# Attention logits and token logits in groups of the TensorE array, second feed-forward product of unsplit fp32 operands

## Chip, cores and metric

The kernel runs on one core of a Trainium2 chip. The metric is the device time in microseconds (us) of one execution; each figure is a median of several runs.

## What is computed

Eight sequences of 750 frames of 192 channels go through four stages. The reference, cut to what matters here:

```python
h = relu(pointwise(depthwise(x)));  h = pairs_max(h)              # 750 -> 375 tokens
h = layernorm(real(fft2(h)))
w = layernorm(h) @ w_qkv                                          # 12 heads of 64
logits = sum((w / norm)**2, -1) * temp;  Pi = softmax(logits)     # "token logits", 12 x 375
h = h - (w * Pi / (1 + sum(Pi * w*w))) @ w_out
probs = softmax(q @ kk.T / 4)                                     # 12 heads of 16, for 56 selected tokens
attn = probs @ v @ Wo;  h2 = layernorm(h) + where(selected, attn, mix)
out = h2 + gelu(n2 @ W1 + bf1) @ W2 + bf2                         # 192 -> 768 -> 192
```

All of it is fp32 in and out.

## The kernel before

The work is pipelined over the eight batches. Each engine has its own instruction stream, and `pipeline` calls `step(p, q, r, w)` ten times in it: batch p is in the front part (convolution, spectrum, token attention), batch q in the middle part (normalisation, scores, routed attention), batch r in the last part (feed-forward), and w is the batch whose depthwise taps VectorE works on ahead of time. Six of the ten steps have a front, a middle and a last batch; below they are "full steps". Step 0 has only a front, step 1 front and middle, step 8 middle and last, step 9 only the last. The order within a step is written out by hand for each engine, and engines wait for one another through semaphores.

The 375 tokens lie in three tiles of 125 partitions or along the free dimension; the 768 inner columns of both feed-forward and token attention are six tiles j of 128.

Where a product needs more precision than one pass, an operand is split into a high and a low part (type fp32r), and three products high·high, high·low and low·high are summed (`split_product`, L1068). An unsplit fp32 product is one call, which the trace shows as two records of matmul.

What the change touches, in the order of a full step:

- `gelus` (ScalarE, L985): after each `forward_up(r, j)` the gelu goes into one of three buffers (L989), then a copy of it becomes the high part (L993). `split_gelu` (GpSimd, L789 to 796) subtracts to get the low part. Between its pieces GpSimd works the `power` calls (L802), the reciprocal roots of the norms, for VectorE.
- On VectorE `spectrum_norm` (L432) and `second_norm` (L444, tile `even`) run meanwhile. TensorE's `front_input(p)` transposes `even` (L1060); ScalarE and VectorE split the result (L879, L451).
- `logits(q, j)` (TensorE, L1248): 96 channels x (2 heads x 64 queries) against 375 keys, six calls. The operand `qb` (VectorE, L618) holds the queries under a mask, so that each call sees only its two heads among six. The results alternate between two PSUM banks, so call j waits for the exponential j-2.
- For each j the loop then runs `qkv(p, j)` (L1126), a `logits` call and `turn(q, j-1)` (L1258, transposes of the probabilities). ScalarE does, per j, the exponential (L962), two copies of the qkv result (L888, L889) and the copy of the turned probabilities (L967). VectorE does the maxima (L625) and two depthwise taps after every second one (L371).
- `forward_down(r, 0, j)` (L1321): three split products per j, for token tile 0. Tiles 1 and 2 follow further down in the step.
- `token_logits(p)` (L1132): six calls of 12 output rows x 375 columns, accumulated in one PSUM region, after `rhead` (VectorE, L463). VectorE takes the maximum (L468) after two more depthwise taps, ScalarE the exponential (L893) after the copy of the last turned tile, VectorE the softmax (L473 to L484), and TensorE spreads the result over the heads (`spread`, L1143).
- `values` (L1266) already puts its products of 32 output rows into three groups of columns of the array.
- `token_out` (L1151): eighteen unsplit fp32 calls of 128 x 125 weights and 192 columns.

In step 0 GpSimd also splits the weights (`split_weight`, L782), `w_2` among them, while VectorE does taps.

## Time and profile before

| | us |
|---|---|
| median of 3 runs | 689.04 (688.39 to 697.84) |
| the profiled execution, its own time | 688.68 |
| its span from first to last instruction | 686.7 |
| TensorE busy in the span | 585.2 (85%) |
| VectorE busy | 475.2 (69%) |
| ScalarE busy | 255.3 (37%) |
| GpSimd busy | 144.4 (21%) |
| chain that ended last: TensorE, VectorE, GpSimd | 51%, 21%, 5% of the span |

The profiled execution lies 0.4 us under the median, and 2.0 us of it lie outside the span. The granted clock of TensorE was 0.925 in the mean: it has two levels, 1.2 and 2.4 GHz, and the profile writes the mean of a stretch as a share of the higher one. The busy time of a group of matmuls counts overlapping records once, so a mean duration is the latency of one record and not what it costs in a row of them; what it costs is read from the starts.

### The profile page before, as it was taken

The numbers are of one execution on the slowest core, as the hardware profiler recorded it, in microseconds if no ns is written. First come the engines' busy times: TensorE is split into PE (matmuls) and PEld (weight loads), VectorE is DVE, ScalarE is ACT, GpSimd is POOL, SyncE is SP. The second block draws the span as 40 slices with busy tenths as digits, with TensorE's granted clock in tenths as the row PEclk, the third lists the DMA queues.
The fourth block names the chain that finished last, engine by engine and source line by source line (L and its number), as shares of the span: only waits on it lengthen the run. The fifth ranks groups of instructions, "written<-read, shape, count | busy, mean of one in ns | idle before, by whom it ended". The sixth has DMA issues, their size and how long they took to land.

```text
span 686.7 us, 9949 instructions
## 1 busy us (share of the span) xinstructions
PE 585.2 (85%) x3488; PEld 470.3 (68%) x3488; DVE 475.2 (69%) x1235; ACT 255.3 (37%) x662; POOL 144.4 (21%) x126
## 2 busy tenths in 40 slices
PE   1536598989989998999899999999899989968975
PEld 1325276759776876787777787678768776866765
DVE  6549767667886888678878878788768573843330
ACT  0013113701474146603671267116721564115431
POOL 5228011002050025002500231032202040023022
PEclk9976698877999999999999999999899999958978
DMA  7420010010001000100000000100000000000000
GB/s 181 117 70 1 0 35 1 1 34 1 1 0 36 17 1 2 35 6 12 0 27 7 17 0 0 34 17 0 0 0 17 1 0 1 18 2 0 1 18 17
DMA packets 8325, 12.50 MB, mean 18 GB/s; under 512 B 1875, under 2 KB 6957, under 8 KB 8296
## 3 DMA queue, kind: packets, MB, share of 16 engines
q1 hardware_dynamic: 8296, 12.12, 6.6%
q8 instruction: 17, 0.28, 0.2%
q14 instruction: 12, 0.10, 0.0%
HBM read 9.81 MB, written 2.30 MB: 18 GB/s over the span
## 4 chain that ended last, share of the span: by engine, by line
PE 51%; DVE 21%; issue 18%; POOL 5%; ACT 3%; DMA 1%; POOLq 0%; DVEq 0%; SPq 0%; ACTq 0%
PE xb L1068 7%; PE yb L1321 6%; PE xb L1151 5%; PE xb L1132 5%; PE zb L1068 5%; PE zb L1248 5%; PE yb L1068 3%; PE xb L1098 3%; PE zb L1258 2%; DVE even L444 2%; POOL gelu_low L795 2%; DVE dw L389 2%; POOL rs L805 2%; DVE st L342 2%; PE xb L1143 2%
## 5 line engine op out<-in xcount | busy, mean ns | idle before, releaser
L805 POOL TENSOR_TENSOR rs<-ve,half 125x3 f32<-125x3 f32 (+1 forms) x32 | 33.6, 1049 | 390.8 <-DVE ve L354 318.1
L371 DVE SCALAR_TENSOR_TENSOR dw<-x_in,w_dw_sb,dw 96x750 f32<-96x750 f32 x84 | 82.7, 1033 | 0.2
L795 POOL TENSOR_TENSOR gelu_low<-gelu,gelu_high 128x375 fp32r<-128x375 f32 x48 | 47.2, 998 | 119.7 <-ACT gelu_high L993 119.5
L1068 PE MATMUL yb<-n2T,w_sb 96*128 96x376 f32 x288 | 64.1, 370 | 5.5 <-DVE n2T L684 5.0
L1068 PE MATMUL xb<-xhT,w_qkv_sb 96*128 96x376 f32 x288 | 64.5, 370 | 1.2 <-DVE xhT L451 1.2
L1068 PEld LDWEIGHTS yb<-n2T,w_sb 96*128 96x128 f32 x288 | 53.5, 208 | 8.4 <-DVE n2T L684 5.7
L1068 PEld LDWEIGHTS xb<-xhT,w_qkv_sb 96*128 96x128 f32 x288 | 53.0, 205 | 5.7 <-DVE xhT L451 3.0
L1151 PE MATMUL xb<-scratch,w_sq 128*125 128x192 f32 x288 | 53.0, 347 | 4.1 <-ACT scratch L900 4.1
L1321 PE MATMUL yb<-w_sb,gelu_high 128*125 128x192 f32 x288 | 53.5, 287 | 2.3 <-POOL gelu_low L795 2.3
L1151 PEld LDWEIGHTS xb<-scratch,w_sq 128*125 128x125 f32 x288 | 51.2, 203 | 5.0 <-DVE scratch L512 4.5
L1321 PEld LDWEIGHTS yb<-w_sb,gelu_high 128*125 128x125 f32 x288 | 44.2, 194 | 8.3 <-issue 5.7
L625 DVE TENSOR_REDUCE nmax<-zb 128x1 f32<-128x375 f32 x48 | 25.6, 544 | 24.8 <-PE zb L1248 24.4
L1248 PE MATMUL zb<-kT,qb 96*128 96x375 f32 x96 | 41.0, 526 | 1.3 <-ACT probs L962 1.3
L1321 PE MATMUL yb<-w_sb,gelu_low 128*125 128x192 f32 x144 | 40.0, 278 | 0.0
L1132 PE MATMUL xb<-w_sq,rhead 128*12 128x375 f32 x96 | 33.9, 505 | 7.1 <-DVE rhead L463 7.1
L967 ACT ACTIVATE probsT<-zb 125x384 f32<-125x384 f32 x48 | 24.9, 518 | 39.8 <-PE zb L1258 39.8
L1098 PE MATMUL xb<-dft_n_sb,pooled_h 125*96 125x376 f32 x96 | 33.8, 504 | 0.9 <-DVE pooled_h L400 0.9
L490 DVE TENSOR_TENSOR w_sq<-w_s,xb 128x376 f32<-128x376 f32 x48 | 25.2, 538 | 11.5 <-PE xb L1143 11.5
L983 ACT ACTIVATE n2T<-zb 96x750 fp32r<-96x750 f32 x8 | 6.3, 791 | 68.1 <-PE zb L1060 68.1
L900 ACT ACTIVATE scratch<-w_out_sb,natt 128x192 f32<-128x192 f32 x24 | 9.2, 445 | 59.9 <-DVE natt L510 59.9
L1258 PEld LDWEIGHTS zb<-ident_sb,probs 128*125 128x125 f32 x144 | 22.5, 187 | 12.9 <-issue 4.8
L1088 PE MATMUL xb<-w_pw_sb,dw 97*125 97x192 f32 x64 | 17.9, 364 | 14.5 <-DVE dw L389 13.9
(188 smaller groups left out, 1269.5 us busy)
## 6 DMA issues: line engine op xcount, KB each, us to landing
x_in<-in_x SPq DMA_DIRECT2D x8, 567.0 KB, 4.2
out<-res_f SPq DMA_DIRECT2D x8, 281.2 KB
probsT<-in_w_qkv SPq DMA_DIRECT2D x1, 576.0 KB, 6.9
w_out_sb<-in_w_out SPq DMA_DIRECT2D x1, 576.0 KB
probs<-in_w SPq DMA_DIRECT2D x1, 576.0 KB
probsT<-in_w SPq DMA_DIRECT2D x1, 576.0 KB, 4.3
rows_sb<-in_rows SPq DMA_DIRECT2D x1, 504.0 KB
dft_n_sb<-in_dft_n SPq DMA_DIRECT2D x1, 493.5 KB
```

The costliest lines, as they stand in the source:

```text
L371: ins = dve.scalar_tensor_tensor(out=dw[0:C, c, :], in0=src, scalar=w_dw[:, c, k:k + 1], in1=dw[0:C, c, :], op0=ALU.mult, op1=ALU.add)
L490: dve.tensor_tensor(u[:, j, :], w_s[:, j, :], xb[:, j % 2, 0:NE], ALU.mult).then_inc(u_done.sem, 1)
L625: dve.tensor_reduce(nmax[:, j:j + 1], zb[:, j % 2, 0:N], AX.X, ALU.max, negate=True).then_inc(qmax_done.sem, 1)
L795: pool.tensor_tensor(gelu_low[:, j, 0:N], gelu[:, j % 3, 0:N], gelu_high[:, j, 0:N], ALU.subtract)\
L805: pool.tensor_tensor(out_[:], in_[:], half3[:] if len(in_.shape) == 3 else half3[:, 0, :], ALU.pow).then_inc(rs.sem, 1)
L1068: ins = mm(o, a[:, k], b[:, l], start=start and k + l == 0, stop=stop and k == 1)
L1098: ins = mm(xb[0:C, c, 0:2 * KF], pooled_h[:, t, chan(c)], dft_n[:, t, :], start=(t == 0), stop=(t == T - 1))
L1132: ins = mm(xb[0:H1, 0, 0:N], rhead[:, j, :], w_sq[:, j, 0:N], start=(j == 0), stop=(j == IT - 1))
L1151: ins = mm(o, u[:, j, tok(t)], w_oa[:, j, :], start=(j == 0), stop=(j == IT - 1))
L1248: mm(zb[:, j % 2, 0:N], qb[:, c, 2 * i:2 * i + 2, :].rearrange("p h q -> p (h q)"), kT[:, c, 0:N], start=True, stop=True).then_inc(ql_read ...
L1258: ins = pe.transpose(zb[0:P, 2 + j % 2, 128 * t:128 * t + 128], probs[:, j, tok(t)], ident[:])
L1321: ins = mm(o, g[:, j, tok(t)], w_2[:, l, j, :], start=(j == 0 and g is gelu_high and l == 0), stop=(j == IT - 1 and g is gelu_low))
```

## The change

The attention logits become two rounds of three calls. A call takes 32 rows of the array (two heads, their real 32 channels) instead of 96 masked ones, and the three calls of a round go to three groups of rows and to three PSUM banks (`score_bank`), two of which are banks that the feed-forward uses. The token logits go to four groups of columns: call j writes the 32 rows of group j % 4, so `rhead`, `head_mask`, the softmax tiles and the selector `head_sel` get 128 rows instead of 12 or 64; high and low part of Pi are now made in one operation on 128 rows. The gelu stays whole in six buffers, and `forward_down` is one fp32 call per j with the unsplit `w_2`; the high and low parts, their copies, subtractions and signals are gone. New waits: a round of `logits` waits for the gelu that read its feed-forward bank, and `forward_down(r, 0, 0)` for all exponentials of q. The diff, cut to its core:

```diff
-        head_sel = sb("head_sel_sb", [64, IT, 128], fp32r)
+        low_rows = sb("low_rows_sb", [128, 1])
+        head_sel = sb("head_sel_sb", [128, IT, 128], fp32r)
-        w_2 = sb("w_2_sb", [128, 2, IT, D], fp32r)
+        w_2 = sb("w_2_sb", [128, IT, D])
-        rhead = sb("rhead", [128, IT, H1])
+        rhead = sb("rhead", [128, IT, 32])
-        qb = sb("qb", [C, CT, H1 // 2, Q])
+        qb = sb("qb", [C, CT, 2, Q])
-        gelu = sb("gelu", [128, 3, NE])
-        gelu_high = sb("gelu_high", [128, IT, NE], fp32r)
-        gelu_low = sb("gelu_low", [128, IT, NE], fp32r)
+        gelu = sb("gelu", [128, IT, NE])
...
+        def score_bank(j):
+            return (zb[:, 0], zb[:, 1], yb[:, 0], yb[:, 1], zb[:, 0], zb[:, 1])[j]
...
             def token_max(b):
-                dve.tensor_reduce(lgm[:, 0:1], xb[0:H1, 0, 0:N], AX.X, ALU.max, negate=True).then_inc(lmax_done.sem, 1)
+                dve.tensor_reduce(lgm[:, 0:1], xb[:, 0, 0:N], AX.X, ALU.max, negate=True).then_inc(lmax_done.sem, 1)
...
+                dve.tensor_copy(pi_high[:], pi[:]).then_inc(pi_steps.sem, 1)
+                dve.wait_ge(*pi_steps.of(b, 5))
                 if not first(b):
                     dve.wait_ge(*pib_ready.before(b))
-                dve.tensor_copy(pi_parts[0:H1, :], pi[:]).then_inc(pi_steps.sem, 1)
-                dve.wait_ge(*pi_steps.of(b, 5))
-                dve.tensor_tensor(pi_parts[32:32 + H1, :], pi[:], pi_parts[0:H1, :], ALU.subtract).then_inc(pi_low_done.sem, 1)
+                dve.scalar_tensor_tensor(out=pi_parts[:], in0=pi_high[:], scalar=low_rows[:], in1=pi[:],
+                                         op0=ALU.mult, op1=ALU.add).then_inc(pi_low_done.sem, 1)
...
-            def split_gelu(b, j0, j1):
...
-                for j in range(j0, j1):
-                    pool.wait_ge(*gelu_high_done.of(b, j + 1))
-                    pool.tensor_tensor(gelu_low[:, j, 0:N], gelu[:, j % 3, 0:N], gelu_high[:, j, 0:N], ALU.subtract)\
-                        .then_inc(gelu_low_done.sem, 1)
...
-                    split_weight(2, w_2, w_2_32)
...
             def gelus(b, j):
                 act.wait_ge(*w1_ready.of(b, j + 1))
-                if j >= 3:
-                    act.wait_ge(*gelu_low_done.of(b, j - 2))
-                act.activation(gelu[:, j % 3, 0:N], yb[:, j % 2, 0:N], ACT.Gelu, bias=b_1[:, j:j + 1]).then_inc(gelu_done.sem, 1)
                 if j == 0 and not first(b):
                     act.wait_ge(*w2_ready.before(b))
-                act.wait_ge(*gelu_done.of(b, j + 1))
-                act.activation(gelu_high[:, j, 0:N], gelu[:, j % 3, 0:N], ACT.Copy).then_inc(gelu_high_done.sem, 1)
+                act.activation(gelu[:, j, 0:N], yb[:, j % 2, 0:N], ACT.Gelu, bias=b_1[:, j:j + 1]).then_inc(gelu_done.sem, 1)
...
             def token_logits(b):
...
                 for j in range(IT):
-                    ins = mm(xb[0:H1, 0, 0:N], rhead[:, j, :], w_sq[:, j, 0:N], start=(j == 0), stop=(j == IT - 1))
+                    g = j % 4
+                    ins = mm(xb[32 * g:32 * g + 32, 0, 0:N], rhead[:, j, :], w_sq[:, j, 0:N], start=(j < 4), stop=(j + 4 >= IT))
...
-            def logits(b, j):
...
+            def logits(b, c, r):
+                if c == 0:
+                    pe.wait_ge(*qb_done.of(b))
+                    pe.wait_ge(*ms_done.of(b))
+                else:
+                    pe.wait_ge(*prob_done.of(b, 2))
+                if r is not None:
+                    pe.wait_ge(*gelu_done.of(r, IT - 1 + c))
+                for i in range(3):
+                    rows32 = slice(32 * i, 32 * i + 32)
+                    ins = mm(score_bank(3 * c + i)[:, 0:N], qb[rows32, c, :, :].rearrange("p h q -> p (h q)"), kT[rows32, c, 0:N],
+                             start=True, stop=True)
+                ins.then_inc(ql_ready.sem, 1)
...
-            def forward_down(b, t, j):
+            def forward_down(b, t, j, q=None):
                 if t + j == 0:
-                    pe.wait_ge(*gelu_low_done.of(b))
+                    if q is not None:
+                        pe.wait_ge(*prob_done.of(q))
                     pe.wait_ge(*gelu_done.of(b))
...
-                for g, l in ((gelu_high, 0), (gelu_high, 1), (gelu_low, 0)):
-                    ins = mm(o, g[:, j, tok(t)], w_2[:, l, j, :], start=(j == 0 and g is gelu_high and l == 0),
-                             stop=(j == IT - 1 and g is gelu_low))
+                ins = mm(o, gelu[:, j, tok(t)], w_2[:, j, :], start=(j == 0), stop=(j == IT - 1))
...
                 if middle:
-                    logits(q, 0)
-                    logits(q, 1)
+                    logits(q, 0, r)
                 for j in range(IT):
                     if front:
                         qkv(p, j)
                     if middle:
-                        if 1 <= j < IT - 1:
-                            logits(q, j + 1)
+                        if j == 2:
+                            logits(q, 1, r)
                         if j:
                             turn(q, j - 1)
                 if last:
                     for j in range(IT):
-                        forward_down(r, 0, j)
+                        forward_down(r, 0, j, q)
```

## Rows read from the trace of the kernel before

**Rows 1.** Stretches: length, busy us (records) per engine, PEclk, DMA share, GB/s

```profile
303.32:374.70 71.38, 67.32 (x438) 54.51 (x437) 57.56 (x152) 31.50 (x83) 14.23 (x13) 1.00 0.05 12
446.10:520.22 74.12, 70.07 (x439) 56.98 (x438) 57.65 (x151) 32.41 (x83) 14.22 (x13) 0.95 0.01 4
520.22:592.97 72.75, 68.74 (x438) 55.59 (x437) 45.70 (x137) 32.14 (x83) 14.25 (x13) 0.98 0.02 5
```

**Rows 2.** Timeline, TensorE, a full step: start, us, line, operation [idle before, releaser]

```profile
341.72 0.84 PE L1060 MATMUL xb<-ident_sb,even 125*96 125x125 f32 x6 [1.82 <-DVE even L444]
...
350.01 0.79 PE L1248 MATMUL zb<-kT,qb 96*128 96x375 f32 x2
...
352.01 0.79 PE L1248 MATMUL zb<-kT,qb 96*128 96x375 f32 x2
...
356.38 3.95 PE L1132 MATMUL xb<-w_sq,rhead 128*12 128x375 f32 x12
360.26 0.59 PE L1258 MATMUL zb<-ident_sb,probs 128*125 128x128 f32 x3
...
363.74 0.61 PE L1143 MATMUL xb<-pi_parts,head_sel_sb 64*128 64x376 f32 x2 [0.94 <-DVE pi_parts L484]
```

**Rows 3.** Timeline, VectorE in step 1 and a full step, GpSimd in the latter

```profile
115.33 1.07 DVE L432 SCALAR_TENSOR_TENSOR res<-res,rs,rows_sb 125x192 f32<-125x192 f32 x3
...
118.84 0.96 DVE L444 TENSOR_SCALAR even<-res,ag,rs 125x192 f32<-125x192 f32 x3 [0.38 <-POOL rs L805]
...
334.36 1.95 DVE L432 SCALAR_TENSOR_TENSOR res<-res,rs,rows_sb 125x192 f32<-125x192 f32 x3
...
338.74 2.92 DVE L444 TENSOR_SCALAR even<-res,ag,rs 125x192 f32<-125x192 f32 x3 [0.38 <-POOL rs L805]
...
338.67 2.87 POOL L795 TENSOR_TENSOR gelu_low<-gelu,gelu_high 128x375 fp32r<-128x375 f32 x3
```

**Rows 4.** Timeline, ScalarE in the loop over j of that full step

```profile
345.19 0.57 ACT L962 ACTIVATE probs<-zb,nmax 128x375 f32<-128x375 f32 x1
...
348.31 0.61 ACT L962 ACTIVATE probs<-zb,nmax 128x375 f32<-128x375 f32 x1
...
350.04 0.65 ACT L962 ACTIVATE probs<-zb,nmax 128x375 f32<-128x375 f32 x1
...
354.95 0.21 ACT L889 ACTIVATION_READ_ACCUMULATOR w_sq<-xb 128x1 f32 x1
```

**Rows 5.** Chain that ended last, forward_down of tile 0: start, us, what

```profile
354.50 1.94 PE yb L1321 x18
```

**Rows 6.** Line view of token_out: min/median/max ns, first and last start

```profile
L1151 PE MATMUL xb<-scratch,w_sq x36: 325/327/346, 303.3 to 309.0; 128*125 128x192 f32 x36
```

**Rows 7.** Timeline, TensorE: `values`, three groups of columns

```profile
360.78 0.86 PE L1266 MATMUL zb<-probsT,v 125*32 125x128 f32 x18
```

**Rows 8.** Timeline, VectorE and ScalarE after the loop over j

```profile
355.78 1.90 DVE L371 SCALAR_TENSOR_TENSOR dw<-x_in,w_dw_sb,dw 96x750 f32<-96x750 f32 x2
...
361.28 0.55 ACT L893 ACTIVATE lg<-xb,lgm 12x375 f32<-12x375 f32 x1
```

**Rows 9.** Timeline, step 0: GpSimd splitting w_2, VectorE

```profile
56.40 2.85 POOL L787 TENSOR_TENSOR w_sb<-probs,w_sb 128x1152 fp32r<-128x1152 f32 x1
...
56.66 7.36 DVE L371 SCALAR_TENSOR_TENSOR dw<-x_in,w_dw_sb,dw 96x750 f32<-96x750 f32 x4
...
72.72 0.54 DVE L468 TENSOR_REDUCE lgm<-xb 12x1 f32<-12x375 f32 x1 [2.19 <-PE xb L1132]
```

**Rows 10.** Step 9: timeline of ScalarE; chain, all three tiles of forward_down

```profile
671.25 0.57 ACT L989 ACTIVATE gelu<-yb,b_sb 128x375 f32<-128x375 f32 x1
...
673.47 7.79 PE yb L1321 x54
```

**Rows 11.** Stretches of step 1, ahead of the spread and behind it

```profile
143.10:145.10 2.00, 0.00 (x0) 0.00 (x0) 1.61 (x6) 0.25 (x2) 0.00 (x0) 1.00 0.00 0
146.00:163.40 17.40, 17.40 (x72) 13.94 (x64) 12.05 (x41) 1.51 (x4) 0.96 (x1) 0.51 0.00 1
```

More of the change, by code:

```diff
@@ L106, in audio_tower @@
         rnrm = sb("rnrm", [128, IT])
-        rhead = sb("rhead", [128, IT, H1])
-        lg = sb("lg", [H1, NE])
-        lgm = sb("lgm", [H1, 4])
-        pi = sb("pi", [H1, NE])
-        pi_parts = sb("pi_parts", [64, NE], fp32r)
+        rhead = sb("rhead", [128, IT, 32])
+        lg = sb("lg", [128, NE])
+        lgm = sb("lgm", [128, 4])
+        pi = sb("pi", [128, NE])
+        pi_high = sb("pi_high", [128, NE], fp32r)
+        pi_parts = sb("pi_parts", [128, NE], fp32r)
         u = w_sq
@@ L246, in audio_tower @@
         qkvs = pieces(w_qkv32, "w_qkv")
-        heads = (pieces(head_mask, "head_mask") + pieces(temp, "temp") + pieces(head_sel32, "head_sel")
+        heads = (pieces(head_mask, "head_mask") + pieces(temp, "temp") + pieces(head_sel32, "head_sel") + pieces(low_rows, "low_rows")
                  + pieces(rows, "rows", slice(2, 8)))
         rests = [x for dst, name in (
-            (w_out, "w_out"), (w_k32, "w_k"), (w_v32, "w_v"), (w_m, "w_m"), (w_2_32, "w_2"), (w_q, "w_q"), (w_o, "w_o"),
+            (w_out, "w_out"), (w_k32, "w_k"), (w_v32, "w_v"), (w_m, "w_m"), (w_2, "w_2"), (w_q, "w_q"), (w_o, "w_o"),
             (b_k, "b_k"), (q_mask, "q_mask"), (parity, "parity"), (pair, "pair"), (fold, "fold"), (later, "later"), (slot, "slot"), (b_1, "b_1"),
             (nsT[C:C + 1, 0, :], "ones_q"), (cxT[C:C + 1, 0, :], "ones_q2")) for x in pieces(dst, name)]
-        MEMSETS, WEIGHTS = 5, 6
+        MEMSETS, WEIGHTS = 5, 5
         SPLIT = MEMSETS + 2 * WEIGHTS
-        FILLS, SELECTORS = 6, 7
+        FILLS, SELECTORS = 5, 6
         FIRST, DFT, NORM, QKV, HEAD, REST = (16 * len(x) for x in (firsts, dfts, norms, qkvs, heads, rests))
@@ L336, in _ @@
             dve.memset(w_s[:, :, N:NE], 1.0).then_inc(consts.sem, 1)
-            dve.memset(pi_parts[:].bitcast(fp32), 0.0).then_inc(consts.sem, 1)
             dve.wait_ge(taps_in.sem, 16)
@@ L462, in token_norms @@
                 dve.wait_ge(*rn2.of(b))
-                dve.tensor_tensor(rhead[:], head_mask[:], rnrm[:].unsqueeze(2).to_broadcast([128, IT, H1]), ALU.mult)\
+                dve.tensor_tensor(rhead[:], head_mask[:], rnrm[:].unsqueeze(2).to_broadcast([128, IT, 32]), ALU.mult)\
                    .then_inc(rhead_done.sem, 1)
@@ L824, in step @@
                     split_weight(1, w_1, w_qkv32)
[L825 to L828 removed]
+                    split_weight(2, w_k, w_k32)
+                    split_weight(3, w_v, w_v32)
+                    split_weight(4, w_mp, w_m[:])
                 if q is not None:
@@ L1444 @@
     head = 2 * np.arange(IT)[None, :] + (p128 // 64)[:, None]
-    sel = np.zeros((64, IT, 128), f)
-    for r in (0, 32):
-        sel[r:r + H1] = (head.T[None] == np.arange(H1)[:, None, None])
+    r32, j6 = np.arange(32), np.arange(IT)
+    mask = ((p128[:, None, None] // 64 == r32 % 2) & (j6[:, None] // 4 == r32 % 4 // 2) & (r32 < 8)).astype(f)
+    sel = np.zeros((4, 32, IT, 128), f)
+    for j in range(IT):
+        sel[j % 4, :, j] = mask[:, j].T
     data = {
@@ L1458 @@
         "w_qkv": tiles(a["L0_attn_w_qkv"], C),
-        "temp": np.broadcast_to(a["L0_attn_temp"][:, 0], (128, H1)),
-        "head_mask": (head[:, :, None] == np.arange(H1)).astype(f),
-        "head_sel": sel,
+        "temp": a["L0_attn_temp"][:, 0][head],
+        "head_mask": mask,
+        "head_sel": sel.reshape(128, IT, 128),
+        "low_rows": -(p128[:, None] % 8 // 4 == 1).astype(f),
         "w_out": tiles(a["L0_attn_w_out"], 128),
```

50 lines of the change are left out of this document (18 added, 32 removed).

## The prediction

> **What bounds the kernel.** I cut the span at the starts of `token_out` and read the stretches first. Three of the six full steps take about 71.4 us (one is shown), with TensorE busy for 67.3 and VectorE for 57.6; two take 74.12 and 72.75, and only these two have a granted clock under 1.00 [rows 1]. So in a full step TensorE is the bound, but not everywhere: the waits of TensorE in such a step name three idle times, and two of them matter here. It waits 1.82 us for `even` ahead of `front_input` and 0.94 us for the softmax ahead of `spread` [rows 2]. Next I read the timelines of the other engines beside these two places, because there the next bound shows.
>
> Ahead of `front_input` VectorE is late: its three L432 take 1.95 us and its three L444 2.92 us. The same six operations took 1.07 and 0.96 us in step 1, where no gelu is split. In the full step GpSimd's subtractions for the low part run in the same microseconds (the last three, 2.87 us from 338.67) [rows 3].
>
> In the loop over j TensorE needs 2.00 us per j (350.01 to 352.01) [rows 2], and ScalarE 1.73 (348.31 to 350.04), back to back [rows 4]. ScalarE starts late and catches up: TensorE is the bound by a little.
>
> **The second product.** Three split records were replaced by one fp32 call of two records. The split ones: 18 records in 1.94 us, 0.323 us per j [rows 5]. `token_out` has exactly the new shape: 36 records start between 303.3 and 309.0, 5.7 / 35 = 0.163 us each, 0.326 per call [rows 6]. The saving on TensorE is nothing, and nothing is lost. What goes is six copies on ScalarE and six subtractions on GpSimd per step; ScalarE's copies lie beside a saturated TensorE and are worth nothing, GpSimd's subtractions are what held VectorE.
>
> **Ahead of `front_input`.** Without them L432 and L444 take the durations of step 1: 0.88 + 1.96 = 2.84 us less. `even`, ready at 341.66, comes at 338.82. What is late next is TensorE itself, free at 341.72 - 1.82 = 339.90. So the stage starts 1.82 us earlier, with 1.08 us of cover.
>
> **The loop over j.** The attention logits are twelve records. A 375-column record of such a product costs 3.88 / 12 = 0.323 us (356.38 to 360.26) [rows 2], so 3.9 us per step. No row shows groups of rows side by side. The nearest is `values`, where groups of columns do run side by side: 18 records of 128 columns in 0.86 us, under 0.05 each, against 0.163 x 128 / 192 = 0.109 for one alone by [rows 6] [rows 7]; with the last record's latency taken off it is close to three at once. Bounds for the two rounds: 1.3 us (full overlap) and 3.9 us (none). I take 1.3, since the nearest row shows it. But TensorE's 2.6 us are hardly seen: ScalarE becomes the bound of this loop. Its run began at 345.19 and ended at 354.95 + 0.21 = 355.16 [rows 4]; it now begins 1.82 us earlier and loses about 0.2 us of gaps, so it ends at about 353.15. VectorE's maxima and taps fit in between.
>
> The new wait of `forward_down(r, 0, 0)` for all exponentials falls here. Behind the last exponential ScalarE has only the two copies of j = 5, somewhat over half of a 1.73 us round, so that exponential ends at about 352.2. The one before it ended 1.73 us earlier, at 350.5; TensorE turns that one and stands from about 351. Behind the wait are the six calls of tile 0 (1.94 us, to 354.2), then `token_logits`. `rhead` would be ready at 353.9: VectorE needed 355.78 - 355.16 = 0.62 us for it [rows 4, 8], and it gets a little larger. So the wait costs 0.3 us. `token_logits` starts at 354.2 instead of 356.38.
>
> **Token logits.** Six calls in four groups of columns: groups 0 and 1 get two calls, so four rounds of records instead of twelve: 4 x 0.323 = 1.3 us instead of 3.88 (bounds: 1.3, and 3.9 if nothing overlaps; the column row [rows 7] is a like case, so I take 1.3). They end at 355.5. The maximum then meets VectorE's two taps, 1.90 us [rows 8], which start behind `rhead` and end at 355.8: here VectorE is level with TensorE. The last `turn` follows at 355.5, and from its start to the token exponential went 361.28 - 360.26 = 1.02 us [rows 2, 8]: the exponential starts at 356.5 instead of 361.28, 4.76 us earlier. Twelve or 128 partitions cost the same, since the 375 columns set the time. The remaining chain to the end of the step is the same operations, so a full step goes from 71.4 to 66.6 us.
>
> **The sum.** Against the profiled execution's 688.68 us (the median is 689.04):
> - six full steps: 6 x 4.76 = 28.6;
> - two of them had a clock fall behind the idle time ahead of `front_input`, worth (74.12 - 71.38) + (72.75 - 71.38) = 4.1 [rows 1]; with that idle time gone I count the 4.1 as won (bounds 0 and 4.1);
> - step 0: GpSimd no longer splits `w_2`, 2.85 us and its copy, beside which four taps took 7.36 us where 1.90 per two is the usual [rows 8, 9]. `rhead` comes 2 to 4 us earlier, I take 3; then the selector's copy and four taps (3.8 us) behind `rhead` outlast the shorter `token_logits`, VectorE ends last, and the maximum moves from 72.72 to about 67.7: 5.0 (bounds 2.5 to 6);
> - step 1: the full step's gain without the 1.82 us, 2.9;
> - step 8: exponentials no longer wait for a logits call each, 1.0 (0 to 1.3);
> - step 9: `forward_down` starts at 671.25 + 0.57 + 0.05 = 671.9 instead of 673.47, and its 54 records took 7.79 us where 3 x 1.94 = 5.8 is the usual [rows 5, 10], behind an idle time that shrinks: 1.6 + 1.9 = 3.5 (1.6 to 3.5).
>
> Together 45.1 us: 688.7 - 45.1 = 643.6 us. The larger selector and mask arrive by DMA while VectorE is still in its first taps, and the two operations that make the parts of Pi replace two of the same length; both cost nothing.
>
> **A rule against it.** The Trainium skill, "TensorEngine Tiling (Array Packing)", Key Properties, says that a change of tiling mode drains the array. In the trace the grouped `values` start at 360.78, before the 0.59 us of the transposes that began at 360.26 are over [rows 2, 7], so no full drain shows at column groups. By the rule, with 0.3 us for each of the two changes around `token_logits` (an estimate from that 0.59 us row), a full step would lose 0.6 us and the sum would be 647.2 us. The Trainium skill, "TensorE: Matmul & The Clock Gate", Part 3, states 3.07 times for four row groups, which no run here shows yet; by it two rounds of three would cost somewhat more than 1.3 us, and under ScalarE's run the sum stays.
>
> **Rivals.**
> - *Row groups don't overlap* (0.12). The second round then puts 1.95 us instead of 0.65 in front of `qkv(p, 3)`; ScalarE has about 0.6 us of slack there, so 0.7 is lost per step, seven times: 648.5 us. For it: no row shows row groups. Against: the column groups.
> - *The clock falls in the loop over j* (0.11), which is now ScalarE's, with TensorE standing for some tenths per j. By the worse of the two steps where it fell there, 2.74 us in each of six steps: 643.6 + 16.4 = 660.0 us. For it: the falls in [rows 1]. Against: those came behind a full 1.8 us of idle time, and the idle times of 0.94 in each step led to none.
> - *The clock stays up behind the softmax of step 1 too* (0.08). It fell there behind 2.0 idle us, and 17.4 us of unbroken work ran at 0.51 [rows 11]. At full clock that is 17.4 x 0.51 = 8.9, so 8.5 us more are won: 635.1 us. The softmax chain stays as long as it was, which speaks against it.
> - *VectorE isn't held by GpSimd* (0.03), so the stage ahead of `front_input` stays: 6 x 1.82 and the 4.1 come back, 658.6 us. [rows 3] speak against it.
> - *Slower* (0.06): the clock falls at this same place, ahead of `spread`, in most full steps. TensorE now stands 1.2 us for the exponentials and, after 5 us of work, about 1.3 us ahead of `spread` instead of 0.94. One fall costs 8.5 us as in step 1, up to 11.4 with the nine calls of `forward_down` (2.9 us) that lie in a full step's stretch; I take 10. Six of them: 643.6 + 60 = 704 us. It decides from five falls of six (45.1 / 10). Against it: 1.82 us of idle time passed without a fall in the steps at 1.00.
>
> **Numbers.** The forecast itself has 0.60. The range must hold the cases at 635 and 660 and the bounds of steps 0 and 9; it leaves out the slower case: 632 to 662 us. Two per cent, 13.8 us, is about what a measurement here can tell from no change. Faster by more: all cases but the last, 0.94. Of the last case's 0.06, half is four or five falls, which end within 2%: 0.03. Slower, with all six: 0.03.
>
> **What would show it.** Right: L444 near 1 us and no `gelu_low`; `front_input` right behind `selected_products`; in the loop ScalarE back to back with exponentials 1.73 us apart; `token_logits` near 1.3 us; full steps near 66.6 us. Wrong: rounds of `logits` near 2 us; L1321 calls other than 0.326 us; a clock under 1.00 in the steps of batches 2 to 7; a token exponential that still waits for TensorE.

## The result

The changed kernel takes 650.24 us in the median (647.86 to 656.77), the kernel before 689.15: a ratio of 0.942, 95% interval 0.932 to 0.953. It is faster, and 650.2 lies inside the range, 6.6 us above the forecast of 643.6. The profiled execution took 647.86 us with a span of 646.0. In another session (e5, below) the same kernel ran between 644.4 and 656.9 us, with mean granted clocks from 0.927 down to 0.905, the longer runs at the lower clocks.

The stretches of the profile after, cut at the starts of `token_out` as in [rows 1]: step 1, a full step, and what follows the last `token_out` (steps 8 and 9). Columns as in [rows 1].

```profile
79.63:153.03 73.40, 64.82 (x341) 51.82 (x341) 51.40 (x136) 22.33 (x66) 6.03 (x5) 0.76 0.06 16
...
221.39:287.94 66.55, 62.54 (x420) 51.86 (x419) 54.31 (x151) 28.68 (x77) 8.40 (x7) 1.00 0.05 14
...
554.18:646.00 91.82, 71.15 (x377) 60.15 (x376) 30.42 (x91) 23.94 (x52) 7.57 (x6) 0.79 0.04 10
```

A full step takes 66.55 us (66.6 was forecast), and in this execution the clock is at 1.00 in all of them but the first, which still holds the end of step 1's stretch at the lower clock (68.37 us, 0.97). The misses lie in the other two lines, where the clock is at 0.76 and 0.79.

TensorE's timeline in the full step that began at 421.07, to be held against [rows 2, 7]:

```profile
457.63 0.84 PE L1046 MATMUL xb<-ident_sb,even 125*96 125x125 f32 x6
458.40 0.58 PE L1237 MATMUL zb<-kT,qb 32*128 32x375 f32 x2
458.41 0.58 PE L1237 MATMUL yb<-kT,qb 32*128 32x375 f32 x1
458.82 0.48 PE L1237 MATMUL zb<-kT,qb 32*128 32x375 f32 x2
...
470.30 2.22 PE L1314 MATMUL yb<-w_sb,gelu 128*125 128x192 f32 x12 [0.92 <-ACT probs L952]
472.45 1.45 PE L1119 MATMUL xb<-w_sq,rhead 128*32 128x375 f32 x12
473.83 0.59 PE L1248 MATMUL zb<-ident_sb,probs 128*125 128x128 f32 x3
...
477.44 0.61 PE L1130 MATMUL xb<-pi_parts,head_sel_sb 128*128 128x376 f32 x2 [1.05 <-DVE pi_parts L485]
...
481.18 0.35 PE L1130 MATMUL xb<-pi_parts,head_sel_sb 128*128 128x376 f32 x1
481.37 0.80 PE L1054 MATMUL zb<-w_mp,nT 97*125 97x192 f32 x6
```

The 1.82 us ahead of `front_input` are gone (no idle time at 457.63). Three records of the attention logits start within 0.01 us, and the next three 0.42 us later: the row groups run side by side. The twelve records of `token_logits` take 473.83 - 472.45 = 1.38 us instead of 3.88. The new idle time is 0.92 us ahead of `forward_down`, where TensorE waits for the exponentials.

VectorE's and ScalarE's timelines in the same step, to be held against [rows 3, 4]:

```profile
452.15 1.08 DVE L433 SCALAR_TENSOR_TENSOR res<-res,rs,rows_sb 125x192 f32<-125x192 f32 x3
...
455.66 0.96 DVE L445 TENSOR_SCALAR even<-res,ag,rs 125x192 f32<-125x192 f32 x3 [0.38 <-POOL rs L799]
...
464.22 0.62 ACT L952 ACTIVATE probs<-yb,nmax 128x375 f32<-128x375 f32 x1
...
465.96 0.65 ACT L952 ACTIVATE probs<-yb,nmax 128x375 f32<-128x375 f32 x1
...
467.70 0.68 ACT L952 ACTIVATE probs<-zb,nmax 128x375 f32<-128x375 f32 x1
```

VectorE has the durations of step 1, and ScalarE's exponentials follow each other every 1.74 us, back to back.

Where the clock fell: stretches of step 1, ahead of `token_logits` and later, and then TensorE's timeline in steps 1 and 8.

```profile
132.50:135.00 2.50, 0.21 (x4) 0.16 (x8) 1.36 (x5) 1.79 (x7) 0.00 (x0) 1.00 0.00 0
...
150.00:155.00 5.00, 5.00 (x17) 4.39 (x17) 4.22 (x19) 1.15 (x3) 0.00 (x0) 0.50 0.01 3
```

```profile
134.79 1.45 PE L1119 MATMUL xb<-w_sq,rhead 128*32 128x375 f32 x12 [2.45 <-DVE rhead L464]
136.17 1.00 PE L1248 MATMUL zb<-ident_sb,probs 128*125 128x128 f32 x3
...
597.00 0.98 PE L1248 MATMUL zb<-ident_sb,probs 128*125 128x128 f32 x3 [1.44 <-ACT probs L952]
...
603.80 3.89 PE L1314 MATMUL yb<-w_sb,gelu 128*125 128x192 f32 x12 [0.20 <-ACT probs L952]
```

In step 1 TensorE stands for 2.45 us, as `rhead` waits for ScalarE; 1.4 us later the three transposes take 1.00 us instead of 0.59, and the clock stays at the lower level until about 156. That is 136.2 - 79.63 = 56.6 us into the step; in [rows 11] it fell behind the softmax, 146.0 - 84.03 = 62.0 us into it. In step 8 the logits are done early, TensorE stands for 1.44 us, and `forward_down` of tile 0 takes 3.89 us instead of 2.22.

### The profile page after: what moved, and what is told of

It reads as the page before. It is cut to its first block, busy times and chain, and to the rows that moved or that the text cites. A ratio compares the mean times of both kernels' runs of the same rounds, so it can differ in the third digit from the quotient of the medians.

```text
span 646.0 us, 9489 instructions
## 1 busy us (share of the span) xinstructions
PE 547.0 (85%) x3344; PEld 449.4 (70%) x3344; DVE 450.1 (70%) x1234; ACT 231.0 (36%) x614; POOL 94.4 (15%) x76
## 4 chain that ended last, share of the span: by engine, by line
PE 58%; DVE 23%; ACT 11%; issue 6%; DMA 1%; POOL 1%; DVEq 0%; ACTq 0%; SPq 0%
PE xb L1138 8%; PE yb L1054 8%; PE zb L1054 7%; PE yb L1314 7%; PE xb L1084 5%; ACT probs L952 3%; PE xb L1093 3%; ACT w_sq L879 2%; DVE dw L390 2%; DVE nr L541 2%; PE zb L1284 2%; ACT w_s L878 2%; DVE st L343 2%; PE zb L1211 2%; ACT probsT L957 2%
## 5 line engine op out<-in xcount | busy, mean ns | idle before, releaser
L372 DVE SCALAR_TENSOR_TENSOR dw<-x_in,w_dw_sb,dw 96x750 f32<-96x750 f32 x84 | 81.0, 1013 | 0.2
L1314 PE MATMUL yb<-w_sb,gelu 128*125 128x192 f32 x288 | 57.4, 344 | 6.3 <-ACT probs L952 5.7
L1314 PEld LDWEIGHTS yb<-w_sb,gelu 128*125 128x125 f32 x288 | 47.7, 193 | 12.7 <-ACT probs L952 7.1
L957 ACT ACTIVATE probsT<-zb 125x384 f32<-125x384 f32 x48 | 26.5, 552 | 27.5 <-PE zb L1248 27.5
L979 ACT ACTIVATE gelu<-yb,b_sb 128x375 f32<-128x375 f32 x48 | 26.7, 571 | 14.8 <-PE yb L1054 13.4
L1130 PE MATMUL xb<-pi_parts,head_sel_sb 128*128 128x376 f32 x48 | 19.0, 452 | 13.7 <-DVE pi_parts L485 12.9
L1248 PE MATMUL zb<-ident_sb,probs 128*125 128x128 f32 x144 | 28.2, 310 | 2.0 <-ACT probs L952 2.0
L878 ACT ACTIVATE w_s<-xb 128x375 f32<-128x375 f32 x48 | 25.5, 531 | 6.0 <-PE xb L1054 5.7
L1084 PEld LDWEIGHTS xb<-dft_n_sb,pooled_h 125*96 125x96 f32 x96 | 15.6, 170 | 15.8 <-issue 14.4
```

What stands on the lines that cost most here:

```text
L372: ins = dve.scalar_tensor_tensor(out=dw[0:C, c, :], in0=src, scalar=w_dw[:, c, k:k + 1], in1=dw[0:C, c, :], op0=ALU.mult, op1=ALU.add)
L878: act.activation(w_s[:, j, 0:N], xb[:, j % 2, 0:N], ACT.Copy)
L957: act.activation(probsT[:, j, :, :], zb[0:P, 2 + j % 2, 0:T * 128].rearrange("p (t q) -> p t q", q=128), ACT.Copy).then_inc(prT_done.sem, 1)
L979: act.activation(gelu[:, j, 0:N], yb[:, j % 2, 0:N], ACT.Gelu, bias=b_1[:, j:j + 1]).then_inc(gelu_done.sem, 1)
L1084: ins = mm(xb[0:C, c, 0:2 * KF], pooled_h[:, t, chan(c)], dft_n[:, t, :], start=(t == 0), stop=(t == T - 1))
L1248: ins = pe.transpose(zb[0:P, 2 + j % 2, 128 * t:128 * t + 128], probs[:, j, tok(t)], ident[:])
```

## The experiments

Theory 1, from the two traces: a full step's gain has two sources that have nothing to do with each other. One is VectorE, which GpSimd no longer slows; the other is `token_logits`. The attention logits' groups give next to nothing, because ScalarE bounds the loop over j. What was lost against the forecast are clock falls behind idle time that the groups opened. Theory 2: all of it is TensorE time saved by the groups. The full step below is from one `token_out` to the next with the clock up. Steps, falls, step 1 and the stretch behind the last `token_out` (steps 8 and 9) are read from the one profiled execution, which for e6 (674.7 us) is the longest of its five.

| kernel | median us (lowest to highest) | full step | steps with a fall, of six | step 1 | steps 8 and 9 |
|---|---|---|---|---|---|
| before | 689.15 (688.39 to 697.84) | 71.38 | 2 | 73.90 | 93.73 |
| changed | 650.24 (647.86 to 656.77) | 66.55 | 0 | 73.40 | 91.82 |
| e1 product alone | 673.32 (662.99 to 678.03) | 69.50 | 0 | 73.87 | 97.75 |
| e2 both groups alone | 687.14 (681.30 to 688.85) | 68.45 | 5 | 73.23 | 103.56 |
| e3 product, attention | 678.63 (676.18 to 682.27) | 69.66 | 0 | 78.89 | 100.77 |
| e4 product, token | 646.81 (646.39 to 647.32) | 66.36 | 0 | 70.89 | 93.71 |
| e5 changed again | 647.54 (644.37 to 656.87) | 66.56 | 0 | 73.27 | 91.73 |
| e6 subtractions back | 663.84 (659.54 to 674.74) | 67.59 | 2 | 73.26 | 99.66 |
| e7 idle filled | 628.53 (628.24 to 630.31) | 66.54 | 0 | 65.11 | 79.81 |
| e8 odd turns | 649.50 (648.98 to 657.11) | 66.44 | 0 | 70.74 | 96.84 |
| e9 filled, whole rows | 629.39 (627.56 to 631.15) | 66.36 | 0 | 65.06 | 81.01 |
| e10 groups, filled | 673.40 (669.71 to 677.37) | 68.46 | 0 | 73.27 | 103.95 |
| e11 odd turns, filled | 623.38 (623.02 to 623.76) | 65.86 | 0 | 64.79 | 79.17 |
| e12 parts back | 675.95 (673.69 to 680.01) | 68.44 | 4 | 73.35 | 96.70 |

A step that only ends a stretch at the lower clock of step 1 isn't counted as one with a fall. The kernel before had medians of 689.2 to 701.0 us in the sessions of these runs, so the step is the better measure. e1 to e4 ran in one session, e5 to e8 in one, e9 to e11 in one.

**The three edits one at a time and in pairs.** The change is cut into the unsplit product, the token logits' groups and the attention logits' groups; each of these kernels leaves one or two of them as before.

e1: the unsplit product alone.

```diff
-                for g, l in ((gelu_high, 0), (gelu_high, 1), (gelu_low, 0)):
+                ins = mm(o, gelu[:, j, tok(t)], w_2[:, j, :], start=(j == 0), stop=(j == IT - 1))
```

> The kernel before with the second feed-forward product alone of unsplit operands (gelu kept once, no high and low copies of it or of the weight, no GpSimd subtractions); both logits as before. Theory 1 (the steady step loses 1.82 us to VectorE taps and relu-max passes that GpSimd's gelu subtractions slow, and step 0 loses some 5 us to the weight's split): step 71.4 to about 69.5, steps 0 and 9 shorter by 5 and 2 us, one or two clock falls fewer: 667 to 672 us. Theory 2 (the whole gain is TensorE time saved by the logits' groups; the product in one record of fp32 costs TensorE what three records of parts cost): 687 to 690 us.

Measured: 673.3 us, 1.3 us above theory 1's range, and a full step of 69.50, 1.88 us less than before; 1.82 were expected. Step 0 is shorter by 3.1 us, but steps 8 and 9 together are 4.0 us longer than before, at a clock of 0.75 instead of 0.81.

e2: both groups, `forward_down` and the gelu as before.

```diff
-                ins = mm(o, gelu[:, j, tok(t)], w_2[:, j, :], start=(j == 0), stop=(j == IT - 1))
+                for g, l in ((gelu_high, 0), (gelu_high, 1), (gelu_low, 0)):
```

> Both logits in groups of the array, the second feed-forward product still of high and low parts with GpSimd's subtractions. Theory 1: the gain of the groups alone, some 3 us in each of six steady steps and no gain in steps 0 and 9: 667 to 673 us, L432 and L444 of before still slow (1.95 and 2.92 us). Theory 2: all of the gain, 648 to 653 us.

Measured: 687.1 us, a ratio of 0.990 with an interval from 0.979 to 1.001: neither theory. A step with the clock up takes 68.45 us, 2.93 less than before, as theory 1 had it; but the six steps took 72.22, 73.38, 70.45, 70.64, 68.45 and 69.14 us, with a clock of 1.00 in the fifth alone. A step with a fall and the one without as stretches, and TensorE's timeline in the former:

```profile
231.43:304.81 73.38, 68.50 (x438) 57.70 (x437) 57.15 (x151) 32.19 (x83) 14.22 (x13) 0.91 0.05 13
...
445.90:514.35 68.45, 62.64 (x438) 52.25 (x437) 57.13 (x151) 31.52 (x83) 14.24 (x13) 1.00 0.01 4
```

```profile
269.87 0.85 PE L1067 MATMUL xb<-ident_sb,even 125*96 125x125 f32 x6 [1.83 <-DVE even L449]
...
271.95 4.13 PE L1075 MATMUL xb<-xhT,w_qkv_sb 96*128 96x376 f32 x12 [0.39 <-DVE xhT L456]
```

The idle time ahead of `front_input` is still there, and right behind it the twelve records of `qkv` take 4.13 us, where they take 2.32 at full clock. Before, the same idle time was followed by a fall in two steps; with grouped logits behind it, in five. Each count is of one execution; the kernel before ran from 689.0 to 701.3 us beside e1 to e4, at mean clocks from 0.925 to 0.904, so its count changes too.

e3: product and attention logits as changed, token logits as before.

```diff
-                    g = j % 4
-                    ins = mm(xb[32 * g:32 * g + 32, 0, 0:N], rhead[:, j, :], w_sq[:, j, 0:N], start=(j < 4), stop=(j + 4 >= IT))
+                    ins = mm(xb[0:H1, 0, 0:N], rhead[:, j, :], w_sq[:, j, 0:N], start=(j == 0), stop=(j == IT - 1))
```

> The changed kernel with the token logits as before (six chained products of 8 output rows, high and low parts in 64 rows), attention logits in row groups and unsplit product kept. Theory 1 (token logits stand on the path of every step, with 2.5 us of TensorE time saved there and about 0.2 us in what follows): 650 + 6 x 2.5 to 2.9, 665 to 669 us. Rival (VectorE's softmax between logits and spread sets the pace, so that a later start is made up by the idle ahead of it, 1.05 us): 656 to 659 us.

Measured: 678.6 us. The step of 69.66 is what theory 1 expected (66.55 + 3.1); the rest of the miss is the clock in step 1, which took 78.89 us at 0.74, and still more in steps 8 and 9, which took 100.77 us at 0.70, 5.5 and 9.0 us more than in the changed kernel. The rival, that VectorE's softmax gives a later start back, is out.

e4: product and token logits as changed, attention logits as before.

```diff
-                    logits(q, 0, r)
+                    logits(q, 0)
+                    logits(q, 1)
```

> The changed kernel with the attention logits as before (one product of 96 rows at a time, in the loop over j, two banks), token logits in groups and unsplit product kept. Theory 1 (ScalarE with 1.74 us per j bounds the loop over j, so TensorE time saved in it is given up as a wait for the exponentials, 0.91 us a step): 648 to 654 us, the loop about as long, no wait of TensorE behind it. Theory 2 (TensorE time saved is time gained, 2.1 to 2.6 us a step): 663 to 667 us.

Measured: 646.8 us, 1.2 us below theory 1's range, and a step of 66.36, 0.2 us shorter than with the groups. So the attention logits' groups cost a little. TensorE's line in this kernel: no wait for the exponentials.

```profile
468.01 2.11 PE L1303 MATMUL yb<-w_sb,gelu 128*125 128x192 f32 x12
470.06 1.45 PE L1114 MATMUL xb<-w_sq,rhead 128*32 128x375 f32 x12
```

Added in this order, the product is worth 1.88 us a step (e1), the token logits 69.50 - 66.36 = 3.14 (e4), the attention logits -0.2, together the 4.83 by the way they are taken. Taken out of the changed kernel one at a time, the product is worth 68.45 - 66.55 = 1.90 (e2) and the token logits 69.66 - 66.55 = 3.11 (e3): the worths hardly depend on one another while the clock is up.

**The changed kernel beside its variants.** e5 is the changed kernel unedited, e6 has GpSimd's six subtractions again, e7 fills idle time of steps 1, 8 and 9, e8 moves work from ScalarE to VectorE.

> The changed kernel as it is, on the same chip and in the same session as the next three: 647 to 652 us where TensorE's clock falls in no steady step, steady steps of 66.5 to 66.6 us. It is the reference for these.

Measured: 647.5 us, as expected, with a wider spread (644.4 to 656.9).

```diff
+                    pool.wait_ge(*gelu_done.of(b, j + 1))
+                    pool.tensor_tensor(spare[:, j, 0:N], gelu[:, j, 0:N], gelu[:, j, 0:N], ALU.subtract).then_inc(spare_done.sem, 1)
```

> The changed kernel, and on GpSimd again six subtractions a sample of the size and at the places of those of before (gelu minus itself into a spare buffer that nothing reads), so that TensorE and ScalarE have the work of the changed kernel. Theory 1 (GpSimd's passes slow VectorE's normalising and relu-max passes that run beside them, and the front input is late by it): L433 and L445 of after from 1.08 and 0.96 us to about 1.95 and 2.9 us, TensorE idle about 1.8 us ahead of the transposes of the front input in each steady step, step 66.55 to 68.4 us where the clock stays up, and the clock falls behind this idle in several steady steps, as in the kernel with groups alone (up to 5 us each): 660 to 680 us. Theory 2 (GpSimd's work is hidden, and the gain of the product came from ScalarE's copies or from TensorE): 648 to 653 us.

Measured: 663.8 us; 48 subtractions that nothing reads, 39.1 us of GpSimd's time in the whole run, cost 16 us. TensorE in one step:

```profile
263.02 0.84 PE L1060 MATMUL xb<-ident_sb,even 125*96 125x125 f32 x6 [1.00 <-DVE even L447]
...
265.10 4.05 PE L1068 MATMUL xb<-xhT,w_qkv_sb 96*128 96x376 f32 x12 [0.39 <-DVE xhT L454]
```

Theory 2 is out. But the idle time is 1.00 us, not 1.82, and the step 67.59, not 68.4: VectorE's two passes took 1.63 and 2.43 us, not 1.95 and 2.9 (e12 shows why).

e7, the edit at one of its places (34 calls in step 1, 49 in step 8 and 10 in step 9; the expectation miscounts the first two):

```diff
+            def keep(n, bank):
+                for _ in range(n):
+                    mm(bank[:, 0:128], ident[:], ident[:], start=True, stop=True)
...
+                if start:
+                    keep(10, bank)
                 if front:
                     token_logits(p)
```

> The changed kernel, and in steps 1, 8 and 9 alone small fp32 products (identity by identity, 128 columns, into a free bank that nothing reads) ahead of the waits where TensorE stands idle, about as many as fit into each: 47 in all in steps 1 and 8, 10 in step 9. The steady steps are the same instructions. Theory (the losses of steps 1, 8 and 9 are clock falls behind idle time, since this activity takes it away): clock at 1.0 in most of these stretches, step 1 from 73.4 to 64 to 68 us, the tail behind the last token_out from 91.8 to 80 to 86 us: 632 to 642 us. Rival (the clock falls whatever TensorE does there, or VectorE's and ScalarE's chains set the pace of these steps, so that a faster TensorE waits longer): 647 to 653 us.

Measured: 628.5 us, ratio to before 0.908 (0.899 to 0.917), better than expected. Step 1 and the stretch behind the last `token_out`:

```profile
79.67:144.78 65.11, 60.90 (x408) 50.33 (x409) 51.10 (x137) 21.66 (x66) 6.02 (x5) 0.95 0.07 19
...
546.79:626.60 79.81, 70.15 (x496) 61.89 (x494) 30.45 (x91) 23.80 (x52) 7.59 (x6) 0.99 0.04 12
```

More products, and 8.3 and 12.0 us less: the clock went from 0.76 and 0.79 to 0.95 and 0.99. The full steps did not move, but for the first: it took 69.36 us instead of 68.37, since one fall is left, 6.8 us from 143.7, where two waits of 0.72 and 1.04 us weren't filled. It is the clock that costs steps 1, 8 and 9 these 20 us, and what TensorE does in the idle time decides it.

e8:

```diff
+                dve.tensor_copy(probsT[:, j, :, :], zb[0:P, 2 + j % 2, 0:T * 128].rearrange("p (t q) -> p t q", q=128))\
+                   .then_inc(prO_done.sem, 1)
```

> The changed kernel with the copies of the turned probabilities of j = 1, 3, 5 on VectorE in place of ScalarE. Theory 1 (ScalarE, with 1.74 us of exponential, copy, square and turned copy per j, bounds the loop over j, which is why the row groups of the attention logits gave nothing): the wait of TensorE for the exponentials ahead of forward_down (0.92 us) goes, and 0.6 to 1.2 us a steady step with it: 642 to 646 us. Rival (the loop is bound by TensorE's own products or by VectorE, which gets 3 x 0.5 us more): 649 to 654 us.

Measured: 649.5 us, a step of 66.44: the rival's number. The timeline shows why; ScalarE had room and waited for VectorE:

```profile
465.11 0.57 ACT L960 ACTIVATE probs<-zb,nmax 128x375 f32<-128x375 f32 x1 [0.50 <-DVE nmax L628]
```

That maximum stood behind two taps (1.90 us) in VectorE's order.

**What the falls and the loop hang on.** e9 is e7 with the attention logits of before; e10 is e2 with the idle time ahead of `front_input` filled (eight calls of `keep`); e11 is e7 and e8 with VectorE's maxima of a round ahead of its taps.

> The kernel of the run with idle time filled, with the attention logits as before (products of 96 rows, one at a time), token logits in groups and unsplit product kept. With the clock held up in steps 1, 8 and 9 the attention logits' groups are priced without the clock. Theory 1 (the groups give nothing, they cost 0.2 us a steady step): steady step 66.35 against 66.55 us, 624 to 628.5 us. Rival (the groups are worth 1 us or more a step where the clock is up, and it was the falls in steps 1 and 8 that hid it): 634 us or more.

Measured: 629.4 us, 0.9 us above theory 1's range and far from the rival's, steps of 66.36. The 0.2 us a step are there again; the totals of e7 and e9 can't be told apart. No gain of the attention logits' groups was hidden by the clock.

```diff
+                if front and last:
+                    pe.wait_ge(*spec_done.of(p))
+                    keep(8, xb[:, 0])
                 if front:
                     front_input(p)
```

> The kernel with both groups and the split product (second feed-forward product of high and low parts, GpSimd's subtractions), and in the steady steps eight small fp32 products (identity by identity, 128 columns, into a bank that nothing reads then) in the 1.83 us in which TensorE waits for the front input. Theory (behind that idle time TensorE enters the loop over j, and there its clock falls: 13.6 us over six steps against 6 x 68.45 us): no falls in the steady steps, steps of 68.4 to 68.9 us, 666 to 676 us. Rival (the clock falls because of the row groups themselves, a third of the array each, whatever TensorE did ahead): falls as often as without the filling, 681 to 690 us.

Measured: 673.4 us instead of e2's 687.1, and no steady step with a fall: 68.46 us in each but the first (70.08), which holds the end of step 1's fall. TensorE ahead of the loop:

```profile
267.44 0.85 PE L1067 MATMUL xb<-ident_sb,even 125*96 125x125 f32 x6
269.52 2.32 PE L1075 MATMUL xb<-xhT,w_qkv_sb 96*128 96x376 f32 x12 [0.39 <-DVE xhT L456]
```

The row groups with the same products behind them caused no fall where TensorE was busy ahead of them.

```diff
-                    if j in (1, 3, 5):
-                        depthwise(w, *taps[1 + j // 2])
+                for c in range(CT):
+                    if middle:
+                        for j in range(3 * c, 3 * c + 3):
+                            attention_max(q, j)
...
+                    depthwise(w, *taps[1 + c])
```

> The kernel with idle time filled (628.5 us), with the turned copies of odd j on VectorE and VectorE's maxima of a round ahead of its depthwise taps. The copies alone gave 0.1 us a step, where the maximum of j = 4 then stood behind a pair of taps for 0.5 us. Theory (ScalarE bounds the loop over j once VectorE's order doesn't): steady step 65.2 to 66.0 us, 622 to 626 us. Rival (VectorE's own work in the loop, 10.4 us with these copies, is as long as the loop): steady step 66.4 to 67 us, 628 to 632 us.

Measured: 623.4 us, the fastest of all, ratio to before 0.901 (0.892 to 0.909); a step of 65.86, 0.68 less than e7. The wait of `forward_down` for the exponentials went from 0.92 us to 0.31:

```profile
459.19 2.21 PE L1328 MATMUL yb<-w_sb,gelu 128*125 128x192 f32 x12 [0.31 <-ACT probs L963]
```

So the loop over j was bound by ScalarE, with VectorE's order close behind it. No run changes VectorE's order alone; but in the changed kernel ScalarE has no idle time in this loop, from 461.10 to 471.47, that another order could have taken away.

e12: the parts of the gelu made again by both engines, and read by nothing.

```diff
+                act.activation(spare_high[:, j, 0:N], gelu[:, j, 0:N], ACT.Copy).then_inc(high_done.sem, 1)
...
+                    pool.tensor_tensor(spare[:, j, 0:N], gelu[:, j, 0:N], spare_high[:, j, 0:N], ALU.subtract).then_inc(spare_done.sem, 1)
```

> The changed kernel, and for each gelu again ScalarE's rounded copy and GpSimd's subtraction, into buffers that nothing reads; TensorE's product stays unsplit. With GpSimd's subtractions alone TensorE stood idle 1.0 us ahead of the front input, not the 1.82 us of before. Theory (ScalarE's copies hold back each subtraction by another half microsecond, so that they come to lie beside VectorE's L445; all of what the unsplit product gives is here and none of it is TensorE's): idle 1.8 us, steady step 68.4 us where the clock stays up, as with groups alone, and falls behind this idle in several steps of 4 to 5 us each: 665 to 690 us. Rival (the missing 0.8 us a step is TensorE's, three records of parts against one of fp32): steady step 67.6 us, 658 to 668 us, idle 1.0 us.

Measured: 675.95 us, and step for step e2's times: 72.34, 73.38, 70.41, 70.68, 68.44 against 72.22, 73.38, 70.45, 70.64, 68.45.

```profile
266.28 0.85 PE L1065 MATMUL xb<-ident_sb,even 125*96 125x125 f32 x6 [1.82 <-DVE even L448]
268.36 4.13 PE L1073 MATMUL xb<-xhT,w_qkv_sb 96*128 96x376 f32 x12 [0.39 <-DVE xhT L455]
```

TensorE's product is unsplit here and split in e2, with the same step. So none of the product's gain in a full step is TensorE's.

The theory's reason, that ScalarE's copies hold the subtractions back until they lie beside VectorE's pass, is not what the traces show. VectorE's second pass and GpSimd's subtractions beside it, and then the last subtraction of step 9, which has neither VectorE nor ScalarE beside it, in e6:

```profile
260.54 2.43 DVE L447 TENSOR_SCALAR even<-res,ag,rs 125x192 f32<-125x192 f32 x3 [0.38 <-POOL rs L809]
260.47 2.38 POOL L800 TENSOR_TENSOR spare<-gelu 128x375 fp32r<-128x375 f32 x3
...
661.35 0.81 POOL L800 TENSOR_TENSOR spare<-gelu 128x375 fp32r<-128x375 f32 x1 [0.22 <-ACT gelu L993]
```

The same in e12:

```profile
263.30 2.93 DVE L448 TENSOR_SCALAR even<-res,ag,rs 125x192 f32<-125x192 f32 x3 [0.38 <-POOL rs L810]
263.23 2.88 POOL L801 TENSOR_TENSOR spare<-gelu,spare_high 128x375 fp32r<-128x375 f32 x3
...
665.02 0.98 POOL L801 TENSOR_TENSOR spare<-gelu,spare_high 128x375 fp32r<-128x375 f32 x1
```

The subtractions lie beside the pass in both, and start 0.07 us ahead of it in both. What differs is the subtraction itself: gelu minus itself, e6's stand-in, takes 0.81 us, gelu minus its high part 0.98, as before. The three passes of VectorE last as long as the three subtractions beside them. The first pass took 1.63 us in e6 and 1.94 in e12, the second 2.43 and 2.93: 0.81 us in all, which is the missing idle time (1.82 - 1.00). So GpSimd's subtractions account for the whole; a run with ScalarE's copies alone was not made.

## Why the prediction was right, and where not

| term | forecast | measured |
|---|---|---|
| six full steps, clock up | 28.6 | 6 x 4.83 = 29.0 |
| clock falls in full steps | 4.1 | 4.9, with a shorter end of step 1's |
| step 0 | 5.0 | 84.03 - 79.63 = 4.4 |
| step 1 | 2.9 | 73.90 - 73.40 = 0.5 |
| step 8 | 1.0 | 65.46 - 67.55 = -2.1 |
| step 9 | 3.5 | 28.23 - 24.25 = 4.0 |
| sum | 45.1 | 40.7 |

Step 9 is counted from its first transposes. The 4.1 us left out a third full step, the first: it took 74.02 us at a clock of 0.96, so [rows 1] do not hold all steps under 1.00. Step 0's 4.4 us hold for these two executions (the token maximum came at 67.95, 67.7 was forecast); in e5's, of the same kernel, step 0 took 82.42 us at a clock of 0.76.

- **The second product at no cost and no gain on TensorE** was right; e12 beside e2 shows it.
- **The 1.82 us ahead of `front_input`** were right (1.88 in e1), and so was their cause. That ScalarE's copies are worth nothing also stands: the 0.82 us between e6 and e12 are the subtractions' own length.
- **Token logits** were right in size, 1.38 us for 1.3, but the step's parts were not: the token exponential came 4.18 us earlier in the step (361.28 - 303.32 = 57.96, now 474.85 - 421.07 = 53.78), not 4.76. 0.5 us of that is the start of `token_logits`, 472.45 - 421.07 = 51.38 us into the step where 354.2 - 303.32 = 50.88 was forecast: the last exponential was later by about 0.35 us, and the six calls of tile 0, put at 1.94 us from [rows 5], took 2.15. They had taken 356.38 - 354.26 = 2.12 before, by the line that the prediction did not read:

```profile
354.26 0.44 PE L1321 MATMUL yb<-w_sb,gelu_high 128*125 128x192 f32 x2
```

  The step came out right because another 0.7 us were won behind the spread, which the sum held at nothing: from the first `spread` to `token_out` 374.70 - 363.74 = 10.96 us before, 487.66 - 477.44 = 10.22 now. Two errors cancelled.
- **The attention logits** were rightly called hardly seen. The forecast's own bounds for the two rounds, 1.3 and 3.9 us, were settled near the lower (a round takes 464.72 - 463.88 = 0.84 us to the next operation's start, two 1.7); what the step's sum leaves for them, 4.76 - 1.82 - (3.88 - 1.3) = 0.36 us, was measured at -0.2 (e4, e9).
- **Steps 1 and 8** are where the prediction failed: its terms carried over a full step's gain and counted the clock as it fell before. In step 1 the clock falls twice, before and after the change. The first fall, ahead of the loop over j and in it, of the kernel before, of the changed one and of e4, which has the attention logits as before:

```profile
115.40:125.70 10.30, 9.88 (x39) 6.99 (x39) 6.26 (x21) 2.18 (x7) 2.25 (x2) 0.50 0.00 0
...
112.30:126.00 13.70, 13.28 (x54) 10.80 (x54) 8.42 (x24) 5.31 (x18) 2.25 (x2) 0.50 0.01 1
...
111.00:121.20 10.20, 9.33 (x37) 6.67 (x38) 6.15 (x21) 2.18 (x7) 2.64 (x3) 0.50 0.00 0
```

  It lasts 13.7 us or more in every kernel that has the row groups and no filling in step 1, and 10.2 to 10.3 in those without row groups (before, e1, e4); why, no run shows. With it the loop is late, TensorE waits 2.45 us for `rhead` instead of 1.40, and `token_logits` starts 134.79 - 79.63 = 55.16 us into the step instead of 137.81 - 84.03 = 53.78. The second fall comes earlier in the chain, as told above, and more work runs at the lower level. e4's step 1 took 70.89 us, 2.5 less than with the row groups, in one execution of each. In step 8 the row groups leave TensorE standing for 1.44 us where it stood for 1.14 before and the clock stayed up; from 597.0 it falls for 10.2 us. The places before:

```profile
137.81 3.95 PE L1132 MATMUL xb<-w_sq,rhead 128*12 128x375 f32 x12 [1.40 <-DVE rhead L463]
...
637.10 0.90 PE L1248 MATMUL zb<-kT,qb 96*128 96x375 f32 x2 [1.14 <-ACT probs L962]
```

  e7 shows what all falls of the first and last steps cost: 20 us. That is not the price of the groups alone. The longest fall of step 8 (20.5 us from 562.9) comes while TensorE waits 3.17 us for VectorE's `n2T`, and before one of 17.1 us began at 603.5, 0.7 us behind the same wait; e1, without any groups, took 97.75 us for steps 8 and 9. The kernel before with its idle time filled was not run. The prediction's rival of the clock in step 1 asked only whether the old fall would stay, not whether it would come sooner.
- **Step 9** went about as forecast: its 36 records took 6.12 us, at full clock, for 5.8.

```profile
621.73:645.98 24.25, 16.45 (x78) 15.59 (x78) 2.53 (x5) 5.52 (x8) 1.42 (x1) 0.83 0.08 24
...
634.58 6.12 PE L1314 MATMUL yb<-w_sb,gelu 128*125 128x192 f32 x36 [0.66 <-ACT gelu L979]
```

- **The slower rival** was a real danger, at another place: in e2 and e12 the clock falls in five and four of six steady steps, at the start of the loop over j. What kept the changed kernel from it is the product's edit, which takes the idle time ahead of the loop away. That was counted as 4.1 us; in the presence of the groups it is 11.9 (six steps of e2 take 424.3 us, of e10 412.3).
- **The total** lies near the 648.5 us of the rival without overlap. That is chance: the rounds do overlap, 0.84 us each, and `token_logits` took 1.38 us. Most of the distance from the forecast lies in steps 1 and 8, as the table shows.

## What to carry to other kernels

An edit that makes one engine faster is worth what the next bound leaves of it, and the idle time it opens can cost more than that: look in each stage, the first and last too, at what TensorE will do in the new gap, since filling it with work that nothing reads gave 19 us (e7) and 13.7 (e10), where the attention logits' groups gave nothing. Two edits can protect each other: in one session the product alone gave 24.5 us (e1), the groups alone 10.7 (e2), product and token logits together 51.0 (e4), against a kernel before that itself ran between 689.0 and 701.3 us there. Where two engines slow each other, put the suspected instruction back with the operands that it had: a stand-in that reads one tile twice was 0.17 us shorter, and gave back 1.04 us of a step instead of 1.89.
